# A two-layer convolution and attention kernel: programs entered on a second pass, one load's columns in uneven row counts, and another order at the end

## The reference

```
patches : q, k = LN(x) @ Wqk_p (1024 x 2048);  v = LN(x) @ Wv_p (1024 x 1024)
          x += (softmax(q k^T) v + dwconv(v)) @ Wout_p (1024 x 1024)
windows : q, k = LN(pooled) @ Wqk_w (1024 x 2048);  v = LN(x) @ Wv_w (16384 x 1024)
          x += (softmax(q k^T) v + dwconv(v)) @ Wout_w (1024 x 16384)
```

## Time and profile before

| | us |
|---|---|
| median of three executions | 747.84 (747.60 to 748.36) |
| the profiled execution, its own time | 747.63 |
| its span, from first to last instruction | 746.4 |
| TensorE matmul busy | 436.4 (58%) |
| VectorE busy | 91.5 (12%) |
| ScalarE busy | 38.2 (5%) |
| mean rate of all transfers | 429 GB/s |

### The profile page before, as it was taken

One profiled execution on the slowest core, in us unless ns is written; L12 is line 12 of the kernel. 1 busy time (PEld: TensorE's weight loads), 2 busy tenths in 40 slices (PEclk: granted clock), 3 DMA queues, 4 the chain that ended last, 5 costly groups with the idle time before them and its releaser, 6 DMA issues.

```text
span 746.4 us, 6667 instructions
## 1 busy us (share of the span) xinstructions
PE 436.4 (58%) x2895; PEld 129.9 (17%) x2895; DVE 91.5 (12%) x254; ACT 38.2 (5%) x80; POOL 9.3 (1%) x21
## 2 busy tenths in 40 slices
PE   7699944444445454454586989445444454544548
PEld 5333200000001111111122332000000011111113
DVE  2765200000002000000005161000000020000000
ACT  2211100000000000000001111000000000000000
POOL 2100000000000000000001000000000000000000
PEclk9689977777767777777788899876776777777779
DMA  9999999999999999999999999999999999999998
GB/s 394 447 394 436 454 415 439 436 443 418 436 446 418 439 433 443 421 432 446 418 439 436 417 434 443 446 418 432 443 432 432 432 446 418 432 443 432 432 415 347
DMA packets 7923, 320.45 MB, mean 429 GB/s; under 512 B 1049, under 2 KB 1585, under 8 KB 2153
## 3 DMA queue, kind: packets, MB, share of 16 engines
q1 hardware_dynamic: 7913, 320.31, 99.5%
HBM read 319.82 MB, written 0.49 MB: 429 GB/s over the span
## 4 chain that ended last, share of the span: by engine, by line
DMA 64%; PE 32%; DVE 3%; ACT 1%; issue 0%; SPq 0%; DVEq 0%; ACTq 0%
DMA ring<-halves 60%; PE bank L485 10%; PE bank L512 9%; PE bank L404 4%; DMA ring<-last 4%; PE bank L421 2%; PE bank L413 2%; PE bank L536 1%; PE bank L341 1%; PE bank L323 0%; PE bank L389 0%; DMA cst<-blurs 0%; DVE ring L722 0%; PE bank L381 0%; PE bank L354 0%
## 5 line engine op out<-in xcount | busy, mean ns | idle before, releaser
L485 PE MATMUL bank<-ring,stage 128*4 128x512 f32 x1024 | 141.4, 714 | 141.1 <-DMA ring<-halves 141.1
L512 PE MATMUL bank<-ring,wf_t 128*32 128x512 f32 x960 | 137.9, 739 | 127.3 <-DMA ring<-halves 127.3
L512 PEld LDWEIGHTS bank<-ring,wf_t 128*32 128x32 f32 x960 | 33.7, 133 | 221.1 <-DMA ring<-halves 121.0
L485 PEld LDWEIGHTS bank<-ring,stage 128*4 128x4 f32 x1024 | 27.0, 97 | 255.1 <-DMA ring<-halves 154.1
L932 DVE TENSOR_TENSOR image<-bank,image 128x32 f32 (+1 forms) x30 | 5.1, 193 | 277.6 <-PE bank L323 277.6
L897 DVE COPY wv_t<-bank 128x32 f32<-128x32 f32 x2 | 0.4, 192 | 287.1 <-PE bank L323 287.1
L323 PE MATMUL bank<-ident,area 128*128 128x128 f32 (+1 forms) x117 | 18.3, 284 | 12.3 <-ACT area L653 11.1
L653 ACT COPY area<-bank 128x512 f32<-128x512 f32 x15 | 8.8, 586 | 281.2 <-PE bank L512 281.2
L404 PE MATMUL bank<-extra,area 128*64 128x512 f32 x64 | 18.2, 734 | 3.3 <-DVE area L806 3.3
L469 PE MATMUL bank<-extra,area 128*64 128x512 f32 x64 | 17.6, 712 | 2.0 <-DVE area L871 2.0
L323 PEld LDWEIGHTS bank<-ident,area 128*128 128x128 f32 (+1 forms) x117 | 12.5, 141 | 30.9 <-ACT area L653 23.8
(11 more groups left out here) (208 smaller groups left out, 217.0 us busy)
## 6 DMA issues: line engine op xcount, KB each, us to landing
extra<-ends SPq DMA_DIRECT2D x4, 4096.0 KB, 16.0
ring<-halves SPq DMA_DIRECT2D x4, 4096.0 KB, 20.3
ring<-last SPq DMA_DIRECT2D x1, 3072.0 KB, 22.1
ring<-last SPq DMA_DIRECT2D x2, 1536.0 KB, 25.5
ring<-last SPq DMA_DIRECT2D x1, 1024.0 KB, 28.6
ring<-last SPq DMA_DIRECT2D x1, 768.0 KB, 29.6
ring<-halves SPq DMA_DIRECT2D x33, 29.4
ring<-images SPq DMA_DIRECT2D x1, 512.0 KB, 3.6
```

What stands on the lines that cost most here:

```text
L485: m = mm(bank[0][32 * j:32 * j + 4, :], stage[:, k // 8, at:at + 4], w[:, j], start=False, stop=False)
L512: m = mm(bank[6 + g][32 * j:32 * j + 32, :], wf_t[:, h, :], w[:, j], start=(h == 0), stop=(h == GROUP - 1))
```

## The change

1. The program of TensorE, ScalarE and VectorE is put into a loop over `visit` of two turns with `If(visit > 0)` around its body: on the first turn the engine jumps over the body to the end and back, on the second it does the work. VectorE's body is in two such parts, one up to the end of the first layer and one for the second.
2. In the second layer the load of half 1 with the small matrices (`load_low_heavy`) has its first 15,616 columns go as one transfer over all 128 rows, and the last 768 columns (3 KB a row) as three transfers of rows 0 to 99, 100 to 119 and 120 to 127. The counts in `half_there` follow.
3. In the second layer TensorE's last full group is no longer written out behind the loop. The loop over groups has all four turns, with an `If` around the second group of each.
4. The narrow pieces are cut at heads 5 and 7 instead of 4 and 7.
5. The old pixels are added with 4 products of 128 columns instead of 16 of 32.
6. The finished rows are stored in six transfers (15, 13, 11, 9, 7 and 1 rows) instead of two of 28.

```diff
-LAST_PIECES = ((0, WIDE, 0, 4), (0, WIDE, 4, 6), (0, WIDE, 6, 8), (WIDE, BANK, 0, 4), (WIDE, BANK, 4, 7), (WIDE, BANK, 7, 8))
+LAST_PIECES = ((0, WIDE, 0, 4), (0, WIDE, 4, 6), (0, WIDE, 6, 8), (WIDE, BANK, 0, 5), (WIDE, BANK, 5, 7), (WIDE, BANK, 7, 8))
...
+        LOW_COLS, LOW_ROWS = 768, ((0, 100), (100, 120), (120, P))
+        ROW_STORES = ((0, 0, 15), (0, 15, LAST), (1, 0, 11), (1, 11, 20), (1, 20, 27), (1, 27, LAST))
...
+            def load_low_heavy(L, t, b):
+                src, at = halves[t * 2 + (L * N_HALVES + 2 + b)], b * HALF * SLOT
+                cols = HALF * SLOT - LOW_COLS
+                sp.dma_start(ring[:, at:at + cols], src[:, 0:cols]).then_inc(half_landed[b], 16)
+                for lo, hi in LOW_ROWS:
+                    sp.dma_start(ring[lo:hi, at + cols:at + HALF * SLOT], src[lo:hi, cols:HALF * SLOT]).then_inc(half_landed[b], 16)
...
-                load_half(L, -1, 1)
+                if L:
+                    load_low_heavy(L, -1, 1)
+                else:
+                    load_half(L, -1, 1)
...
-            for wy in range(2):
-                sp.dma_start(out[wy], out_rows[wy * WIN:wy * WIN + LAST, :]).then_inc(rows_stored, 16)
+            for wy, lo, hi in ROW_STORES:
+                sp.dma_start(out[wy, lo:hi], out_rows[wy * WIN + lo:wy * WIN + hi, :]).then_inc(rows_stored, 16)
...
+            with pe.Fori(0, 2) as visit:
+                with pe.If(visit > 0):
...
-                with pe.Fori(0, TURNS - L) as i:
-                    for g in range(2):
-                        group(L, i, g)
-                        turn_group(i * 2 + (2 * TURNS * L + g + 1), g)
+                        with pe.Fori(0, TURNS) as i:
+                            group(L, i, 0)
+                            turn_group(i * 2 + (2 * TURNS * L + 1), 0)
+                            with pe.If(i + L < TURNS):
+                                group(L, i, 1)
+                                turn_group(i * 2 + (2 * TURNS * L + 2), 1)
...
-            group(1, TURNS - 1, 0)
             last_piece(0)
-            turn_group(4 * TURNS - 1, 0)
             last_piece(1)
...
-                for j in range(4):
-                    if s8 < 3:
-                        mm(bank[7][32 * j:32 * j + 32, s8 * P:s8 * P + P], residual[:, s8, j, :], ident, start=False, stop=False)
-                    else:
-                        mm(bank[6][32 * j:32 * j + 32, 0:P], residual[:, s8, j, :], ident, start=True, stop=False)
+                dst = bank[7][:, s8 * P:s8 * P + P] if s8 < 3 else bank[6][:, 0:P]
+                mm(dst, residual[:, s8].rearrange("p j w -> p (j w)"), ident, start=(s8 == 3), stop=False)
...
+            with act.Fori(0, 2) as visit:
+                with act.If(visit > 0):
...
+            with dve.Fori(0, 2) as visit:
+                with dve.If(visit > 0):
+                    first()
+                    layer(0)
+                with dve.If(visit > 0):
+                    layer(1)
```

More of the change, by code:

```diff
@@ L249, in stores_landed @@
         def stores_landed(sp):
-            sp.wait_ge(rows_stored, 16 * 3)
+            sp.wait_ge(rows_stored, 16 * (len(ROW_STORES) + 1))
             sp.wait_ge(last_stored, 16)
@@ L335, in first_there @@
                     half_there(L, None, s // HALF)
[L338 to L371, removed]
@@ L723, in _, with first @@
[L723 to L732 removed]
+            def first():
+                dve.wait_ge(images_landed, 16)
+                v.tensor_tensor(l0_sq[:, :, :], l0_in[:, :, :], l0_in[:, :, :], ALU.mult).then_inc(squared, 1)
+                dve.wait_ge(blurs_landed, 16)
+                v.tensor_tensor(blocks_x[:, :, :].rearrange("p b (x c) -> p (b x) c", c=C), cc("taps_x").unsqueeze(2).to_broadcast([P, 5 * XM, C]),
+                                cc("same_c").unsqueeze(1).to_broadcast([P, 5 * XM, C]), ALU.mult).then_inc(blocks_built, 1)
+                dve.wait_ge(blurred_y2, 1)
+                v.tensor_copy(l0_blur[:, 1, BANK:2 * BANK], bank[3][:, :]).then_inc(blur2_copied, 1)
+                mean_c = area[6][:, :]
+                dve.wait_ge(mean_sq, 1)
+                then(v.tensor_copy(mean_c, bank[5][:, :]))
+                for i, (sq, fields) in enumerate(((7, 2), (0, 4))):
+                    dve.wait_ge(field_ready, fields)
+                    dve.wait_ge(mean_sq, i + 1)
+                    then(v.tensor_tensor(l0_part[:, i], bank[sq][:, :], l0_part[:, i], ALU.subtract))
+                    v.tensor_scalar(l0_part[:, i], l0_part[:, i], 0.0, None, ALU.max).then_inc(l0_var, 1)
+                    if i == 0:
+                        dve.wait_ge(l0_std, 1)
+                        then(v.tensor_scalar(l0_part[:, 0], l0_part[:, 0], EPS, None, ALU.add))
+                        then(v.reciprocal(l0_part[:, 0], l0_part[:, 0]))
+                work = l0_blur[:, 0, 0:BANK]
+                dve.wait_ge(field_ready, 5)
+                then(v.tensor_tensor(work, bank[4][:, :], mean_c, ALU.subtract))
+                then(v.tensor_tensor(work, work, l0_part[:, 0], ALU.mult))
+                dve.wait_ge(l0_std, 2)
+                then(v.scalar_tensor_tensor(work, l0_part[:, 1], EPS, work, ALU.add, ALU.mult))
+                dve.wait_ge(pads_zeroed, 1)
+                v.tensor_tensor(pixels.rearrange("p y x -> p x y"), work.rearrange("p (x y) -> p x y", y=IMG),
+                                bank[6][:, :].rearrange("p (x y) -> p x y", y=IMG), ALU.add).then_inc(image_ready, 1)
@@ L766, in softmax, with layer @@
                 return v.tensor_tensor(x, x, wide(2), ALU.mult)
-            for L in range(2):
+            def layer(L):
                 vv = vec[:, L, :]
```

508 lines of the change are left out of this document (256 added, 252 removed).

## The result

The changed kernel takes **752.48 us** (median of 6 runs, 751.86 to 753.26) against 747.78 us of the kernel before on the same chip (6 runs, 747.60 to 748.36): a ratio of 1.0063 [1.0053, 1.0074], 4.7 us slower. The forecast was 747.2, the range 746.2 to 748.6; it missed on the slow side. The profiled execution took 752.94 us, with a span of 751.7; before it was 747.63 with 746.4.

A forecast was written before the change was run, and what follows sets the result against it. The prediction took one DMA queue, busy 99.5% of the span, to bound the kernel. Evening −0.8, start 0, between the layers 0, TensorE's end +0.2 and stores 0 gave −0.6 us: median 747.2 us, range 746.2 to 748.6.

The forecast's parts named there:

- The low-heavy load: Second layer's uneven load: ten engines get up to 13 rows, six none; 0.8 us gain, from 0.57 loss to 1.6 gain.
- the evening: Sixteen transfer engines finish unevenly at the end; making them finish together gives about 1 us, at most 1.6.
- the late engines are not those that are relieved: Rival: a late engine gets 13 rows, 0.57 us later; 748.6 us, or 747.9; chance 0.27, shared with no effect.
- The two-pass programs: Early jumps fetch instruction blocks before loads saturate; 0, bound 0.5 us gain; VectorE's start 0 to 3.6 us late, hidden.
- The starved queue: Rival: jumps at the start or between layers run the queue empty; 2.4 us beyond cover, 750 us; above 749.3, chance 0.09.
- Between the layers: Tightest place of the queue, next load issued at 419.5 us: added tests cost 0.2 us together, 0 on the time.
- TensorE's end: Last group's turn waits 0.88 us for ScalarE's copy, pieces recut, fewer identity products: +0.2 us, bounds −0.2 and +0.9.
- Six stores: Six row stores for two keep SP busy 2.3 us, hidden behind the last product: 0, bound 0.3 us.
- The sum: All terms added: −0.6 us, giving 747.0 us for the profiled execution and 747.2 for the median.
- The list of what would show it: Profile signs at the start and end, such as DMA share near 1.0 until the last narrow piece lands, before 743 us.

The follow-up runs named there:

- run 10: Kernel before, last 768 columns of the second layer's half-1 load as two transfers, even rows and odd rows: 747.73 us, 1.0000.
- run 6: Kernel before, the same 768 columns in three transfers of 48, 48 and 32 rows: 749.76 us, 1.0032.
- run 9: Kernel before, the same 768 columns in two transfers, rows 0 to 63 and 64 to 127: 750.57 us against 747.72, 1.0038.
- run 3: Kernel before with only the low-heavy load (100, 20 and 8 rows) added: 750.50 us, 1.0038.
- run 7: Kernel before, transfers of 100, 20 and 8 rows in the last load of half 0 near 695 us, plain load between the layers: 750.53 us, 1.0037.
- run 13: Kernel before, the 768 columns in twelve spread transfers of ten rows each, then rows 120 to 127: 750.32 us against 747.71, 1.0036.
- run 4: Changed kernel without two-pass loops and without the low-heavy load; TensorE's new end and the six stores remain: 748.08 us, 1.0004.
- run 2: Changed kernel with the plain load in place of the low-heavy load: 748.85 us, 1.0015.
- run 11: Kernel with only TensorE's new end and the six stores, plus the two-pass loop on TensorE alone: 747.72 us against 747.72, 0.9999.
- run 1: Changed kernel without the two-pass loops: 750.84 us against 747.70, 1.0043.
- run 12: Kernel with only TensorE's new end and the six stores, plus the two-pass loop on VectorE alone: 748.17 us, 1.0006.
- run 16: Kernel before with transfers of 100, 20 and 8 rows over the last 384 columns instead of 768: 749.05 us against 747.90, 1.0012.

## Why the prediction was wrong

**The step that failed** is *The low-heavy load*: "After the shift 742.6 and 742.6 to 743.0 ... I take 0.8 us of gain from a range between 0.57 us of loss ... and 1.6 us of gain." It counted bytes of each engine at 27.1 GB/s, whatever rows these bytes went to, and put the price of dealing them to other rows at nothing. Measured is +2.8 us, five times the worst bound. It also took the evening as a gain, and the last landing moved the other way.

*Two parts of the 2.8 us.* The landings of the second of the six last pieces tell them apart. Changes are against the kernel before, in us; one execution each.

| 768 columns dealt as | rows for each engine | mean landing | last landing | first to last |
|---|---|---|---|---|
| before | all alike | | | 2.1 |
| even, odd rows (run 10) | all alike | +0.1 | +0.1 | 2.0 |
| 48, 48, 32 (run 6) | all alike | +2.0 | +2.1 | 2.2 |
| 64, 64 (run 9) | all alike | +3.0 | +3.3 | 2.4 |
| 100, 20, 8 (run 3) | 13, 12 or none | +2.0 | +2.7 | 3.8 |
| 100, 20, 8, late (run 7) | 13, 12 or none | +2.0 | +2.8 | 3.7 |
| twelve of 10, 8 (run 13) | 13, 12 or none | +1.7 | +2.7 | 3.7 |

The mean moves because packets take longer. In the third run the packets of 3, 61 and 32 KB around the uneven load take together 1.9 us of all sixteen engines longer. That is the larger part, and the prediction had nothing for it. Where the engines carry unlike numbers of rows, the last landing moves 0.7 to 1.0 us further than the mean. That is the prediction's own rival, "the late engines are not those that are relieved", with its 0.57 us: some late engines were relieved, but the last was not. The trace does not name the engine of a packet, so that the last ones are among those with 13 rows is inferred from this growth. The premise of the evening, that the engines finish unevenly, was right.

*What stands in its place.* An engine's bytes do not cost the same whatever rows they go to. Shown: the cost follows the bytes, not the number of transfers or the packets' size; it depends on which rows move together (low and high 2.8 us, even and odd 0); it occurs with a deep queue as well; and the packets themselves take longer (3 KB in 187 to 245 ns instead of 122). Argued from this: it is the ways into the rows that are shared; each set of rows has a way of its own that takes about what one engine gives, 27.1 GB/s. In a transfer with all 128 rows each engine uses one way and all are full. When 100 rows are dealt to ten engines, several queue at one way, while others have no taker. With twelve spread transfers ten engines write to all ways while the six others already write the next load to ways of their own; there too some get more than they can take. In the ninth run, where sixteen engines would share eight ways, a packet of 3 KB takes 245 ns, just twice the 122. No counter here shows a way directly, and since source and destination rows change together in every run, a crowding on the side of HBM is not excluded by any of them.

The rates fit: over long stretches both kernels stay at 433 or 434 GB/s (400 to 700 us and 60 to 400), and none of the versions goes above that there. The Trainium skill, page "DMA: Bandwidth & Descriptors", section "Where 436 GB/s comes from", puts it down to sixteen ports of SBUF, 435.2 GB/s together, and names the ports, not the engines, as the limit; 433 agrees. The same section gives a lower limit, some 358 GB/s, for loads from HBM; the loads of this kernel run at 433, so that figure does not hold here. The same page, section "The descriptor swizzle", says that each engine of a 128-row transfer writes to one port, and that the low 64 rows lie on the even ports, the high ones on the odd. By that rule a transfer of rows 0 to 63 has half of the ports, and one of even rows has all; the ninth run (2.8 us) and the tenth (0) agree in which of the two costs. Half of the ports explains the doubled packets of 3 KB, 1.0 us; why the loads around them lose 2.0 us more is not worked out. The prediction cited this page for how many engines take part and not for where they write.

If this is the cause, dealing better would not repair the idea: to relieve an engine, others must write its rows, and at a full queue that way has no room beside its owner. The twelve spread transfers (+2.6 us) agree with it. They fail for the second reason as well: their landings are as far apart as those of the third run.

**The two-pass programs**, taken as 0 with "bound 0.5 us of gain" and up to 3.6 us of lateness hidden. VectorE's lateness was forecast rightly (first product at 7.11, "before 8 us"), the load behind the first image's result at 30.1 ("before 33"). Not all of it was hidden: 0.8 us by the medians alone, 1.6 beside the low-heavy load, and the profile shows 1.7 at the issue at 386.85 (one execution each; in the kernels without a loop on VectorE that issue lies anywhere between 384.0 and 386.0, so the 1.7 is worth no more than a sign). The saving did not exist: a block of 16 KB is still fetched behind 700 us, and there are eight instead of seven. (The new end of the program alone, in the fourth run, has six; with the loops, in the second, it has eight.) What went wrong is the size of the cover. It was worked out for the one load that waits for the first image, while the landings ahead of it (the images', 3.6 to 5.0 us from issue) grew too. The starved queue of the rival (above 749.3) has the right sign for the start, but 60 to 400 us run at 434 GB/s in both kernels, and it gives only this smaller part; its 2.4 us did not come.

**Between the layers**, 0: right as far as the queue goes. The next issue follows the load by 34.4 us as before (421.29 − 386.85, 419.5 − 385.1), and the seventh run puts the same loss elsewhere.

**TensorE's end**, +0.2 with bounds −0.2 and +0.9. The shape was right: 0.72 us of wait for the copy (0.88 forecast), no wait for the narrow pieces. The end alone, with the stores, measured 748.08 against 747.70, +0.4 and not distinguishable from 0. From the end of the last group to the last product the forecast had 744.70 − 733.43 = 11.27 us, and measured are 749.74 − 738.53 = 11.21. That is partly luck, for two errors cancel: the forecast carried along the 0.64 us for which the first narrow piece's weights had waited for a transfer, which fell away, and it had nothing for the 0.68 us of "issue" behind the turn. This "issue" is 0.68 to 0.71 us in the runs with a two-pass loop on TensorE (the changed kernel, runs 2 and 11) and 0.46 to 0.51 in those without (runs 1, 4 and 12), so some 0.2 us of it belong to that loop. The last group takes 9.61 us instead of 9.22, but that goes with the clock and not with the change: with the same end of the program it takes 8.90 us at a mean granted clock of 0.80 (run 2) and 9.94 at 0.71 (run 4), and here 9.61 at 0.74 against 0.76 in the kernel before.

**Six stores**, 0: issued at 746.27 in 2.16 us and done 1.3 us before the last product's end; right.

**The sum.** 2.8 (load) + 0.8 (two-pass) + 0.4 (end and stores) = 4.0 of 4.7 us. The remaining 0.7 appear only when load and loops are together. One reading is that each exposes what the other hid; no run separates this, and it stays open. Of the loops' 0.8 us, too, no single engine's loop showed a part that can be told from 0.

**The list of what would show it.** "The DMA share should stay near 1.0 until the last narrow piece lands": it was 0.43 in 745 to 750. "That landing should come before 743 us": it came at 747.87. "The prediction is wrong if ... TensorE begins the last group later than at 724.4": 728.92. The share, the other test, was of no use: in 420 to 428 us it is 0.98 in the changed kernel, where the rate is 291, and 0.89 in the kernel before, which fails that test itself.

## What to carry to other kernels

Where one saturated queue sets the time, keep each transfer's rows as the other transfers have them: all 128 on the same sixteen engines. To even out the engines one must know which are the last; the trace here gives landings but no names. Before rows are dealt out by hand, ask not only which engine carries a byte but which rows it moves and who else uses them at that moment, and try it with one even cut and one uneven cut of the same bytes. And read GB/s beside the DMA share: packets that take up to twice as long keep the share at 0.92 to 0.98 while the rate falls to between 241 and 321 GB/s.

## What the runs showed of the hardware

- 384 KB in transfers over parts of the rows cost 2.1 us (48, 48, 32 rows), 2.8 (100, 20, 8; and 64, 64) or 2.6 (ten engines, rows spread) in a full queue; with even and odd rows, or all rows, 0.
- The slow packets are not only those of the small transfers (3 KB in 187 to 245 ns instead of 122): in the runs with such transfers packets of 32 KB of the load behind them took as much as 2.8 us instead of 1.2 (run 1; 1.7 at most in run 16, with half of the bytes).
- The sixteen engines land a transfer 2.1 us apart in the kernel before, and 3.6 to 3.8 us apart behind the loads of 100, 20 and 8 rows.
- Thirteen issues on SP took 9.64 us in the run with the spread rows, 0.74 us each. Others: 0.33 us for a whole load, 0.43 for 128 rows of 768 columns, 0.36 each for 100, 20 and 8 rows, 0.59 each for two of 64 rows, neighbouring or alternating. No run separates what makes the 0.74.
- A jump over TensorE's program at the start brought two early blocks of 16 KB and removed none later (eight in runs 2 and 11, six in run 4); the 8 KB packets that came early with ScalarE's and VectorE's loops were on another queue and cost nothing that shows.
